# Transposes of a unit grouped over three PSUM banks, and two groups of heads at once in the halves of the partitions: a two-layer gated cross-attention kernel on one core

## The chip, the core and the metric

The kernel runs on one NeuronCore of one Trainium2 chip. The metric is the device time of one execution in microseconds (us), a median over runs. A core has TensorE (PE in the profile, its weight loads PEld), VectorE (DVE), ScalarE (ACT), GpSimd (POOL) and SyncE (SP, which here only issues DMAs). Each runs its own instruction stream in order, and they meet at semaphores.

## The reference, cut to what matters

```python
x = x + tanh(g_xattn[0]) * L0_xattn(layernorm(x), ctx, ...)          # "first attention"
x = x + tanh(g_ffn[0])   * L0_ffn(layernorm(x), ...)
x = x + tanh(g_xattn[1]) * L1_xattn(layernorm(x), ctx, ctx, ...)     # "second attention"
x = x + tanh(g_ffn[1])   * L1_ffn(layernorm(x), ...)
# L0_xattn: 2 batches, 256 queries, keys = 512 context rows + 256 latents, 32 heads of 128, 8 key heads,
#   q and k rms-normed; probs = softmax(q k^T / sqrt(128)); out = probs v; out @ Wo
# L1_xattn: 2 batches, 256 queries, 512 keys, 32 heads of 16, 8 key heads (4 heads share one);
#   softmax(q k^T / 4) v; out @ Wo
```

## The kernel before, in words

Matrices that need fp32 exactness are split into a high and a low part (hi by ScalarE, lo = value - hi by VectorE or GpSimd) and multiplied as three single-pass products (`mm3`, L70).

**First attention (`attn0`).** A loop of 8 turns g, one for each key head, which serves 4 query heads. In a turn a *unit* u is one query head h = u // 2 with one batch b = u % 2, 8 units. In iteration u of `attend` (L590) TensorE runs, in this order: at even u the transposes of the next head's queries ("q", 4 transposes into one bank), at odd u from 3 on the transposes that spread a head's softmax factors ("r", 4 of them), then the scores of unit u + 1 (12 matmuls), then three times four transposes of the probabilities of unit u ("p") followed by six matmuls with the values for unit u - 1 (`times_v`, L578). All groups of transposes go through two banks `tbank` in turn: a group c waits until VectorE has emptied the bank of group c - 2 (L536). ScalarE copies the high part out of the bank (L290) and takes the exponentials (L316), in the written order p, exp, p, exp, [o], p (L322 to L335), where o is the high part of a finished head's output (L310), at odd u from 3 on. VectorE takes row maxima (L443), subtracts for the low part (L430, L432) and scales a head's output with its factors (`normalise_o`, L452). The values' sums of a head alternate between two banks `obank`. GpSimd works through a fixed list in each turn (L223): low part of output 0 (L205), split of Wo, low part of output 1, split of the next turn's Wq (L183, L185), split of Wkv, and so on. TensorE's first projection of the next turn (`project_q`, L510) comes right after `attend` and waits for that split of Wq (L512).

**Second attention (`attn1`).** Here the contraction of a score is only 64 rows long: 16 dimensions times high and low parts of q and k. Rows 64 to 127 of `kS` and `qS` hold zeros (L780, L791), so each matmul covers 128 rows. A unit is one head and one batch, 64 units in all, in 4 turns of 16. For each TensorE makes the scores (2 matmuls of 512 columns, L1472) for the maxima (L1419); then it makes them again transposed, with the negated maxima added through an identity (4 + 4 matmuls of 256 columns, L1484 and L1489), which ScalarE exponentiates (L1400). Every fourth unit it multiplies four units with the values, in four groups of 32 columns of the array (L1503, 32 instructions of 256 columns), and transposes the result (L1512). ScalarE copies that result (L1390), VectorE divides it (L1441, L1443). `scores(n + 1)` stands ahead of `scores_T(n)` in TensorE's order (L1515 to L1525).

## Time and profile before

| | us |
|---|---|
| median of 3 runs | 1085.82 (1079.99 to 1086.55) |
| the profiled execution | 1088.03 |
| its span, first to last instruction | 1086.2 |
| TensorE busy | 1005.9 (93% of the span) |
| VectorE busy | 632.7 (58%) |
| ScalarE busy | 501.4 (46%) |
| GpSimd busy | 359.8 (33%) |
| mean granted TensorE clock | 0.975 of full speed |

Busy time is the time an engine spends in instructions, with waits left out. TensorE's matmuls are pipelined, so a matmul of 256 columns shows some 280 ns but starts some 117 ns after the one ahead of it: distances between starts tell its throughput, durations do not.

### The profile page before, as it was taken

What the parts mean: (1) busy time and instruction counts of PE and PEld (TensorE: products, weight loads), DVE (VectorE), ACT (ScalarE), POOL (GpSimd) and SP (SyncE); (2) the same over time, 40 slices, a digit from 0 to 9 for tenths busy, and PEclk for the clock granted to TensorE, in tenths of its full rate; (3) what the DMA queues carried; (4) which work ended last, traced back from release to release, by engine and by line L of the source; (5) the groups of instructions that cost most, each with busy time, mean ns of one, the idle gap of its engine ahead of it and who ended that gap; (6) DMA issues with size and microseconds to landing.
All of it is one profiled execution on the core that took longest, in us unless ns stands there. A gap on an engine that the chain in (4) does not pass through costs nothing. (4 is left out here: it accounts for less than half of the span.)

```text
span 1086.2 us, 18566 instructions
## 1 busy us (share of the span) xinstructions
PE 1005.9 (93%) x6748; PEld 878.6 (81%) x6748; DVE 632.7 (58%) x1102; ACT 501.4 (46%) x968; POOL 359.8 (33%) x246
## 2 busy tenths in 40 slices
PE   4899999999999999999999999999899969999975
PEld 3888989898898989889898898989677857777654
DVE  6566457556546745754674574567347736666464
ACT  4356337435534643653473374346145125555423
POOL 3307403720830371083046126305147308000041
PEclk9989999999999999999999999999999989999987
DMA  6001100200200110020011003000053072221001
GB/s 213 2 1 62 37 1 9 88 0 0 90 6 0 38 59 0 0 97 0 0 58 39 0 0 116 0 1 1 26 179 116 1 237 56 54 53 34 2 0 39
DMA packets 31409, 46.49 MB, mean 43 GB/s; under 512 B 3472, under 2 KB 15376, under 8 KB 31376
## 3 DMA queue, kind: packets, MB, share of 16 engines
q1 hardware_dynamic: 30800, 46.03, 13.6%
q8 instruction: 22, 0.36, 0.1%
q14 instruction: 11, 0.09, 0.0%
q10 hardware_dynamic: 576, 0.00, 0.0%
HBM read 41.83 MB, written 4.19 MB: 42 GB/s over the span
## 5 line engine op out<-in xcount | busy, mean ns | idle before, releaser
L430 DVE TENSOR_TENSOR ptL<-tbank,ptH 128x512 fp32r<-128x512 f32 x192 | 132.3, 689 | 84.0 <-ACT ptH L290 84.0
L290 ACT ACTIVATE ptH<-tbank 128x512 fp32r<-128x512 f32 x192 | 115.7, 603 | 109.5 <-PE tbank L539 109.2
L205 POOL TENSOR_TENSOR oTL<-o_norm,oTH 128x512 fp32r<-128x512 f32 x32 | 41.3, 1290 | 349.9 <-ACT oTH L310 349.9
L539 PE MATMUL tbank<-ident,probs 128*128 128x128 f32 x864 | 132.1, 275 | 16.5 <-DVE ptL L430 12.1
L443 DVE TENSOR_REDUCE negmax<-score 128x1 f32<-128x768 f32 x128 | 119.5, 949 | 19.9 <-PE score L74 19.9
L316 ACT ACTIVATE probs<-score,negmax 128x768 f32<-128x768 f32 x128 | 115.6, 904 | 15.5 <-DVE negmax L443 15.5
L72 PE MATMUL obank<-ptH,vH 128*128 128x256 f32 x384 | 122.3, 318 | 0.0
L401 DVE TENSOR_REDUCE sumsq<-probs 128x2 f32<-128x256 f32 (+1 forms) x80 | 42.0, 526 | 135.5 <-ACT probs L285 71.8
L539 PEld LDWEIGHTS tbank<-ident,probs 128*128 128x128 f32 x864 | 97.7, 140 | 26.5 <-DVE ptL L430 14.9
L74 PE MATMUL obank<-ptH,vL 128*128 128x256 f32 x384 | 108.8, 283 | 0.0
L1419 DVE TENSOR_REDUCE a_negmax<-a_score 128x1 fp32r<-128x512 f32 x128 | 82.3, 685 | 45.3 <-PE a_score L1472 44.5
L74 PE MATMUL score<-wkvH,kvT_lo 128*128 128x256 f32 x384 | 108.7, 283 | 0.0
L73 PE MATMUL score<-wkvL,kvT_hi 128*128 128x256 f32 x384 | 108.7, 283 | 0.0
L72 PE MATMUL score<-wkvH,kvT_hi 128*128 128x256 f32 x384 | 108.6, 283 | 0.0
L73 PE MATMUL obank<-ptL,vH 128*128 128x256 f32 x384 | 108.4, 282 | 0.0
L200 POOL TENSOR_TENSOR rnorm<-sumsq,neg_half 128x2 f32<-128x2 f32 (+1 forms) x80 | 71.4, 896 | 107.4 <-DVE sumsq L403 107.3
L1400 ACT ACTIVATE a_exp<-a_scoreT 128x1024 f32<-128x1024 f32 x64 | 65.6, 1025 | 60.2 <-PE a_scoreT L1489 60.2
L72 PE MATMUL score<-kTH,qTH 128*128 128x512 f32 (+1 forms) x256 | 92.4, 361 | 0.6 <-DVE kTL L430 0.6
L74 PE MATMUL score<-kTH,qTL 128*128 128x512 f32 (+1 forms) x256 | 87.2, 341 | 0.0
L73 PE MATMUL score<-kTL,qTH 128*128 128x512 f32 (+1 forms) x256 | 87.2, 341 | 0.0
L72 PEld LDWEIGHTS obank<-ptH,vH 128*128 128x128 f32 x384 | 73.6, 192 | 0.5
L72 PEld LDWEIGHTS score<-wkvH,kvT_hi 128*128 128x128 f32 x384 | 73.7, 192 | 0.3
(246 smaller groups left out, 2417.6 us busy)
## 6 DMA issues: line engine op xcount, KB each, us to landing
wqo_stage<-in_wq SPq DMA_DIRECT2D x9, 1024.0 KB, 5.6
wqo_stage<-in_wo SPq DMA_DIRECT2D x8, 1024.0 KB, 5.2
wkv_stage<-in_wkv SPq DMA_DIRECT2D x9, 512.0 KB, 6.4
a_qS<-q_scratch SPq DMA_DIRECT2D x24, 128.0 KB, 3.6
ctx_stage<-in_ctxT SPq DMA_DIRECT2D x2, 1024.0 KB, 12.5
kS<-k_scratch SPq DMA_DIRECT2D x32, 64.0 KB, 2.1
q_scratch<-qpart SPq DMA_DIRECT2D x16, 128.0 KB, 1.9
wqo_stage<-in_down_w SPq DMA_DIRECT2D x3, 512.0 KB, 3.5
```

The costliest lines, as they stand in the source:

```text
L72: pe.matmul(out, a[0], b[0], start=start, stop=False)
L73: pe.matmul(out, a[0], b[1], start=False, stop=False)
L74: return pe.matmul(out, a[1], b[0], start=False, stop=stop)
L200: pool.tensor_tensor(rn[:, GRP * it:GRP * it + n], ss[:, GRP * it:GRP * it + n], S.neg_half[:, 0:n], ALU.pow).then_inc(rn_done, 1)
L290: act.activation(out, tbank[c % 2][:], ACT.Copy, scale=scale).then_inc(t_hi, 1)
L316: act.activation(probs[:, m % NP, :], score[m % 2][:, 0:SKV], ACT.Exp, bias=negmax[:, m:m + 1], accum_out=rsum[:, m:m + 1]).then_inc(s_exp, 1)
L401: dve.tensor_reduce(ss[:, a:a + n], sq[:, it % 3, 0:n], AX.X, ALU.add).then_inc(ss_done, 1)
L430: i = dve.tensor_tensor(out, tbank[c % 2][:], f32(hi), ALU.subtract)
L443: dve.tensor_reduce(negmax[:, m:m + 1], score[m % 2][:, 0:SKV], AX.X, ALU.max, negate=True).then_inc(s_max, 1)
L539: i = pe.transpose(tbank[c % 2][:, n * P:(n + 1) * P], block_in, S.ident[:])
L1400: act.activation(expo[:, v % NE_, :], scoreT[v % 2][:], ACT.Exp).then_inc(s_exp, 1)
L1419: dve.tensor_reduce(negmax[:, 2 * (v % 2) + t:2 * (v % 2) + t + 1], score[t][:], AX.X, ALU.max, negate=True).then_inc(s_max, 1)
```

## The change

In the first attention the banks for transposes become three and `obank` one. The three groups of transposes of a unit follow each other, then come the three groups of matmuls with the values. The factors ("r") of a head move from odd u from 3 on to even u from 2 on, beside "q", with ScalarE's copy of them. A group of transposes now waits for the last user of its own bank (`place`, `user`): q has bank 1, r has bank 2, p has bank n % 3. Some waits and VectorE's order change with it, `NPT` goes from 4 to 5, and the last factors go ahead of the last matmuls with the values. GpSimd's low part of output 2 moves ahead of the split of Wkv.

In the second attention group 2i lies in rows 0 to 63 and group 2i + 1 in rows 64 to 127. A step m now holds one head of each, 32 steps. Score matmuls and the transposed ones take 64 rows each, written in pairs for the two halves and into different banks; the identity matmuls stay at 128 rows. `scores` has three banks, negated maxima a ring of 16; values are multiplied in two halves, one in each step; the loops are written out; the zero fills are gone; keys and queries of a turn are loaded a whole turn ahead, those of turn 1 ahead of the last feed-forward's weights. Cut to its core:

```diff
-    NP, NPT = 4, 4
...
-    tbank = [ps(f"tbank{i}", [P, 512], fp32) for i in range(2)]
-    obank = [ps(f"obank{i}", [P, 512], fp32) for i in range(2)]
+    tbank = [ps(f"tbank{i}", [P, 512], fp32) for i in range(3)]
+    obank = ps("obank", [P, 512], fp32)
+    wbank = [obank, tbank[2]]
...
-        if u % 2 == 1 and u >= 3:
-            order.append(("r", (u - 3) // 2))
+        if u % 2 == 0 and u:
+            order.append(("r", u // 2 - 1))
...
+    lows = {name: i for i, name in enumerate(name for name in order if name[0] != "r")}
+    TL = len(lows)
+
+    place = [n if kind == "p" and n < CH else {"p": n % CH, "q": 1, "k": c % 2, "r": 2}[kind] if c else 0
+             for c, (kind, n) in enumerate(order)]
+    user = [max((i for i in range(c) if place[i] == place[c]), default=None) for c in range(TC)]
...
+                o_lo_part(g, 2)
                 pool.wait_ge(pe_kv, NKV * g + NKV)
                 split_wkv(g + 1)
-                for h in range(2, GRP):
-                    o_lo_part(g, h)
+                o_lo_part(g, 3)
...
-                act.wait_ge(t_lo, TC * g + at["r", h] + 1)
+                act.wait_ge(o_scaled, GRP * g + h + 1)
...
-                    if u % 2 == 1 and u >= 3:
-                        factors(g, (u - 3) // 2)
+                    if u % 2 == 0 and u:
+                        factors(g, u // 2 - 1)
...
+                    if u % 2 == 1 and u >= 3:
+                        normalise_o(g, (u - 3) // 2)
                     if u + 1 < U:
                         maximum(g, 2 * u + 2)
                     if u % 2 == 0 and u // 2 + 1 < GRP:
                         lo_q(g, u // 2 + 1)
-                    if u % 2 == 1 and u >= 3:
-                        normalise_o(g, (u - 3) // 2)
                     if u + 1 < U:
                         maximum(g, 2 * u + 3)
+                    if u % 2 == 1:
+                        reciprocals(g, u // 2)
                     for c in range(CH * u, CH * u + CH):
                         lo(g, ("p", c), ptL[:, c % NPT, :], ptH[:, c % NPT, :])
-                    if u % 2 == 1:
-                        reciprocals(g, u // 2)
...
-                if c >= 2:
-                    pe.wait_ge(t_lo, TC * g + c - 1)
+                if name == ("p", 2):
+                    pe.wait_ge(t_lo, TL * g + lows["q", 1] + 1)
+                elif user[c] is not None:
+                    last_user = order[user[c]]
+                    if last_user in lows:
+                        pe.wait_ge(t_lo, TL * g + lows[last_user] + 1)
+                    else:
+                        pe.wait_ge(t_hi, TC * g + at[last_user] + 1)
...
-                if u % 2 == 0 and j == 0 and h >= 2:
-                    pe.wait_ge(t_lo, TC * g + at["r", h - 2] + 1)
-                pe.wait_ge(t_lo, TC * g + at["p", c] + 1)
+                if u % 2 == 0 and j == 0 and h:
+                    pe.wait_ge(o_scaled, GRP * g + h)
...
-                    if u % 2 == 1 and u >= 3:
-                        transpose_factors(g, (u - 3) // 2)
+                    if u % 2 == 0 and u:
+                        transpose_factors(g, u // 2 - 1)
                     if u + 1 < U:
                         scores(g, u + 1)
                     for j in range(CH):
                         transpose_probs(g, u, j)
-                        if u:
+                    if u:
+                        for j in range(CH):
                             times_v(g, u - 1, j)
             def finish_units(g):
+                transpose_factors(g, GRP - 1)
                 for j in range(CH):
                     times_v(g, U - 1, j)
-                transpose_factors(g, GRP - 1)
...
-            pool.memset(f32(S.kS[64:P, :, :]), 0.0).then_inc(k_zeroed, 1)
...
-            pool.memset(f32(S.qS[64:P, :, :, :]), 0.0).then_inc(S.q_zeroed, 1)
...
+    vcol = sb("a_vcol", [P, 2, 2, B * SCT, VW], fp32)
+    NX = 4
+    expo = sb("a_exp", [P, NX, 2, 2, 2, SQ], fp32)
...
+    NB = 3
...
+    obank = ps("a_obank", [P, 512], fp32)
...
+    NV = B * GRP
+    NM = NV * TURNS
+    NW = NM // 2
+    STACK = 16 * 16
+    half_rows = [slice(0, P // 2), slice(P // 2, P)]
...
+            for i in range(1, TURNS):
+                if i >= 2:
+                    sp.wait_ge(pe_sT, 2 * NV * (i - 1))
                 for s in range(2):
-                    sp.wait_ge(pe_sT, NU * i - U + U * s)
-                    S.load_k(sp, 2 * i + s, s)
-                    load_q(2 * i + s, s)
+                    S.load_k(sp, i, s)
+                    load_q(i, s)
+                if i == 1:
+                    ffn.loads(sp)
...
+            def exp(m, h):
+                act.wait_ge(pe_sT, 2 * m + h + 1)
+                if m >= NX and h == 0:
+                    act.wait_ge(pe_pv, (m - NX) // 2 + 1)
+                act.activation(expo[:, m % NX, h].rearrange("p s k q -> p (s k q)"), scoreT[h][:], ACT.Exp).then_inc(s_exp, 1)
+
+            def copy_o(w):
+
+                act.wait_ge(pe_pv, w + 1)
+                act.activation(o_quad[:, w % 2, :], obank[:, 0:SQ], ACT.Copy).then_inc(o_copied, 1)
+            for m in range(NM):
+                exp(m, 0)
+                if m % 2 == 1 and m >= 3:
+                    copy_o((m - 3) // 2)
+                exp(m, 1)
+            copy_o(NW - 1)
...
+            def windows(i):
+                for s in range(2):
+                    g = 2 * i + s
+                    dve.tensor_copy(vcol[:, i % 2, s, :, 0:D1], v_rows[:, :, g * D1:(g + 1) * D1]).then_inc(win, 1)
...
+            def maxima(m):
+
+                for e in range(4 * m, 4 * m + 4):
+                    dve.wait_ge(pe_s, e + 1)
+                    dve.tensor_reduce(negmax[:, e % 16:e % 16 + 1], score[e % NB][:], AX.X, ALU.max,
                                       negate=True).then_inc(s_max, 1)
...
+            windows(0)
+            maxima(0)
+            for m in range(NM):
+                if m % 2 == 0 and m >= 4:
+                    finish((m - 4) // 2)
+                if m + 1 < NM:
+                    maxima(m + 1)
+                if m % NV == 1 and m // NV + 1 < TURNS:
+                    if m // NV:
+                        dve.wait_ge(pe_pv, 4 * (m // NV))
+                    windows(m // NV + 1)
+            finish(NW - 2)
+            finish(NW - 1)
...
+            def scores(m, t):
+
+                i, b, j = unit(m)
+                if t == 0 and m % NV == 0:
+                    pe.wait_ge(stack_in[i % 2], STACK * (i // 2 + 1))
+                if t == 0 and m == GRP:
+                    pe.wait_ge(S.late_in[0], STACK // 2)
+                q = b * SQ + t * P
+                for s, rows in enumerate(half_rows):
+                    e = 4 * m + 2 * t + s
+                    if e >= NB:
+                        pe.wait_ge(s_max, e - NB + 1)
+                    pe.matmul(score[e % NB][:], qS[rows, i % 2, j, q:q + P], kS[rows, i % 2, b * SC:(b + 1) * SC],
+                              start=True, stop=True).then_inc(pe_s, 1)
+
...
+            def scores_T(m, h):
+
+                i, b, j = unit(m)
+                if m:
+                    pe.wait_ge(s_exp, 2 * (m - 1) + h + 1)
+                for k in range(2):
+                    key = b * SC + (2 * h + k) * P
+                    for s, rows in enumerate(half_rows):
+                        pe.matmul(scoreT[h][:, 512 * s + k * SQ:512 * s + (k + 1) * SQ], kS[rows, i % 2, key:key + P],
+                                  qS[rows, i % 2, j, b * SQ:(b + 1) * SQ], start=k == 0, stop=False)
+                pe.wait_ge(s_max, 4 * m + 4)
                 for t in range(2):
...
+                    for s in range(2):
+                        c = (4 * m + 2 * t + s) % 16
+                        x = pe.matmul(scoreT[h][:, 512 * s:512 * (s + 1)].rearrange("p (k q) -> p k q", k=2)[:, :, t * P:(t + 1) * P],
+                                      negmax[:, c:c + 1].to_broadcast([P, P]),
+                                      ident_r[:].unsqueeze(1).to_broadcast([P, 2, P]), start=False, stop=t == 1)
                 x.then_inc(pe_sT, 1)
...
+            def times_v(w, h):
+
+                i, b = w // 4, w % 4 // 2
+                if h == 0:
+                    pe.wait_ge(win, 2 * i + 2)
+                    if w:
+                        pe.wait_ge(o_step, 2 * w)
+                pe.wait_ge(s_exp, 2 * (2 * w + 1) + h + 1)
+                for k in range(2):
+                    for c in range(GRP):
+                        s, m = c // 2, 2 * w + c % 2
+                        x = pe.matmul(obank[VW * c:VW * (c + 1), 0:SQ], vcol[:, i % 2, s, b * SCT + 2 * h + k, :],
+                                      expo[:, m % NX, h, s, k, :], start=h == 0 and k == 0, stop=h == 1 and k == 1)
+                if h == 1:
+                    x.then_inc(pe_pv, 1)
+
...
+            for m in range(NM):
+                if m + 1 < NM:
+                    scores(m + 1, 0)
+                scores_T(m, 0)
+                if m >= 2:
+                    times_v((m - 2) // 2, m % 2)
+                if m + 1 < NM:
+                    scores(m + 1, 1)
+                scores_T(m, 1)
+                if m % 2 == 1 and m >= 3:
+                    transpose_o((m - 3) // 2)
+            for h in range(2):
+                times_v(NW - 1, h)
+            transpose_o(NW - 1)
...
+                    at, g = 64 * s + D1 * n, 2 * i + s
```

## Rows read from the trace of the kernel before

**Rows 1.** Windows by stage: stretch, its length, busy time of PE, PEld, DVE, ACT, POOL, PEclk, DMA
```profile
0.00:770.00 770.00, 722.81 (x4931) 660.23 (x4932) 453.69 (x782) 376.30 (x795) 279.18 (x173) 0.99 0.10 32
885.80:1027.50 141.70, 137.92 (x1184) 105.93 (x1184) 89.53 (x169) 71.76 (x80) 23.16 (x21) 0.97 0.26 62
1027.50:1086.20 58.70, 41.49 (x168) 29.31 (x168) 28.09 (x60) 17.90 (x33) 15.49 (x20) 0.81 0.05 18
```
**Rows 2.** Timeline of PE, iteration 1 of turn 4: start, us, engine, line, what
```profile
443.14 0.60 PE L539 MATMUL tbank<-ident,probs 128*128 128x128 f32 x4
443.49 0.36 PE L72 MATMUL obank<-ptH,vH 128*128 128x256 f32 x1
443.69 0.28 PE L73 MATMUL obank<-ptL,vH 128*128 128x256 f32 x1
...
444.29 0.60 PE L539 MATMUL tbank<-ident,probs 128*128 128x128 f32 x4
```
**Rows 3.** Timeline of PE: three of its stalls, in brackets, with who ended them
```profile
440.55 0.66 PE L539 MATMUL tbank<-ident,probs 128*128 128x128 f32 x4 [0.81 <-DVE ptL L430]
...
482.95 0.50 PE L72 MATMUL score<-wqH,kvT_hi 128*128 128x512 f32 x1 [1.73 <-POOL wqL L185]
...
769.27 0.47 PE L72 MATMUL obank<-woH,oTH 128*128 128x512 f32 x1 [3.56 <-POOL oTL L205]
```
**Rows 4.** Windows: iterations 0 and 1 of turn 4, and its `attend` whole
```profile
435.72:440.96 5.24, 4.22 (x29) 3.47 (x28) 3.88 (x6) 2.74 (x6) 0.00 (x0) 1.00 0.00 0
440.96:446.59 5.63, 5.63 (x45) 5.37 (x44) 4.35 (x6) 4.10 (x10) 0.00 (x0) 1.00 0.00 0
...
sum 47.23, PE 43.78 PEld 40.89 DVE 33.34 ACT 30.45 POOL 18.96; mean PE 5.47 PEld 5.11 DVE 4.17 ACT 3.81 POOL 2.37
```
**Rows 5.** Timeline of turn 4: an exponential of iteration 0; iteration 3's transposes p and their emptying
```profile
440.75 0.91 ACT L316 ACTIVATE probs<-score,negmax 128x768 f32<-128x768 f32 x1
...
455.16 0.60 PE L539 MATMUL tbank<-ident,probs 128*128 128x128 f32 x4
...
455.80 0.60 ACT L290 ACTIVATE ptH<-tbank 128x512 fp32r<-128x512 f32 x1 [1.94 <-PE tbank L539]
...
458.52 0.65 ACT L310 ACTIVATE oTH<-o_norm 128x512 fp32r<-128x512 f32 x1
...
459.04 0.61 ACT L290 ACTIVATE ptH<-tbank 128x512 fp32r<-128x512 f32 x1
...
459.69 0.69 DVE L430 TENSOR_TENSOR ptL<-tbank,ptH 128x512 fp32r<-128x512 f32 x1 [1.19 <-ACT ptH L290]
```
**Rows 6.** Timeline of POOL, turn 4
```profile
459.24 1.30 POOL L205 TENSOR_TENSOR oTL<-o_norm,oTH 128x512 fp32r<-128x512 f32 x1 [36.12 <-ACT oTH L310]
...
474.66 3.60 POOL L183 TENSOR_TENSOR wqH<-wqo_stage,zero 128x2048 fp32r<-128x2048 f32 x1 [2.04 <-DMA wqo_stage<-in_wq]
478.34 4.56 POOL L185 TENSOR_TENSOR wqL<-wqo_stage,wqH 128x2048 fp32r<-128x2048 f32 x1
```
**Rows 7.** Timeline, second attention: values' block, then the next unit
```profile
941.44 1.93 PE L1503 MATMUL a_obank<-a_exp,a_vcol 128*32 128x256 f32 x32
...
943.30 0.74 PE L1472 MATMUL a_score<-kS,a_qS 128*128 128x512 f32 x2
...
943.84 1.29 DVE L1419 TENSOR_REDUCE a_negmax<-a_score 128x1 fp32r<-128x512 f32 x2 [2.54 <-PE a_score L1472]
943.88 0.40 PE L1484 MATMUL a_scoreT<-a_ident_r,a_negmax 128*128 128x256 f32 x2
...
944.11 0.40 PE L1489 MATMUL a_scoreT<-a_qS,kS 128*128 128x256 f32 x2
```
**Rows 8.** Page, costliest groups: ScalarE's exponentials of the second attention
```profile
L1400 ACT ACTIVATE a_exp<-a_scoreT 128x1024 f32<-128x1024 f32 x64 | 65.6, 1025 | 60.2 <-PE a_scoreT L1489 60.2
```
**Rows 9.** Timeline of PE: the second attention's first identity matmuls and last values' block
```profile
888.78 0.63 PE L1484 MATMUL a_scoreT<-a_ident_r,a_negmax 128*128 128x256 f32 x2
...
1024.03 1.93 PE L1503 MATMUL a_obank<-a_exp,a_vcol 128*32 128x256 f32 x32 [1.20 <-ACT a_exp L1400]
```

More of the change, by code:

```diff
@@ L1386, in _ @@
         def _(act):
-            def copy_o(r, c):
-                act.wait_ge(pe_pv, r + 1)
-                act.activation(o_quad[:, c, :], obank[c][:, 0:SQ], ACT.Copy).then_inc(o_copied, 1)
-            def turn(i, first, last):
-                for v in range(NU):
-                    n, r = NU * i + v, QUADS * i + v // GRP
-                    if v % GRP == 2 and (not first or v >= GRP):
-                        copy_o(r - 1, (v // GRP - 1) % 2)
-                    act.wait_ge(pe_sT, n + 1)
-                    if v % GRP == 0 and (not first or v >= NE_):
-                        act.wait_ge(pe_pv, r - 1)
-                    act.activation(expo[:, v % NE_, :], scoreT[v % 2][:], ACT.Exp).then_inc(s_exp, 1)
-            turns(act, turn)
-            copy_o(QUADS * TURNS - 1, 1)
+            def exp(m, h):
[12 more added lines that the diff above has]
+            copy_o(NW - 1)
             for t in range(RT):
@@ L1422, in turn @@
-            def turn(i, first, last):
-                for v in range(NU):
-                    n, r = NU * i + v, QUADS * i + v // GRP
-                    if not (last and v == NU - 1):
-                        maxima(n + 1, (v + 1) % NU)
-                    if v % GRP == 3 and (not first or v >= GRP):
-                        finish_quad(i, r - 1, v // GRP - 1)
-                    if v == 4 and not first:
-                        dve.wait_ge(pe_pv, QUADS * i)
-                        window(2 * i + 1, 1)
-                    if v == 12 and not last:
-                        dve.wait_ge(pe_pv, QUADS * i + 2)
-                        window(2 * i + 2, 0)
@@ L1446, in _ @@
             dve.wait_ge(ones_set, 1)
-            window(0, 0)
-            window(1, 1)
-            maxima(0, 0)
-            turns(dve, turn)
-            finish_quad(TURNS - 1, QUADS * TURNS - 1, QUADS - 1)
+            windows(0)
[9 more added lines that the diff above has]
+                    windows(m // NV + 1)
@@ L1460, in _ @@
         def _(pe):
-            def scores(n, v, i):
-                s, b, j = unit(v)
-                if v % U == 0:
-                    pe.wait_ge(stack_in[s], STACK * i + STACK)
-                if isinstance(i, int) and i == 0 and b == 1 and j == 0:
-                    pe.wait_ge(S.late_in[s], 64)
-                for t in range(2):
-                    if not (isinstance(n, int) and n == 0):
-                        pe.wait_ge(s_max, 2 * n + t - 1)
-                    q = b * SQ + t * P
-                    pe.matmul(score[t][:], qS[:, s, j, q:q + P], kS[:, s, b * SC:(b + 1) * SC],
-                              start=True, stop=True).then_inc(pe_s, 1)
@@ L1511, in transpose_o @@
+            def transpose_o(w):
+                pe.wait_ge(o_copied, w + 1)
                 for t in range(2):
-                    x = pe.transpose(obank[c][:, SQ + t * P:SQ + (t + 1) * P], o_quad[:, c, t * P:(t + 1) * P], S.ident[:])
+                    x = pe.transpose(obank[:, SQ + t * P:SQ + (t + 1) * P], o_quad[:, w % 2, t * P:(t + 1) * P], S.ident[:])
                 x.then_inc(pe_oT, 1)
-            def turn(i, first, last):
-                for v in range(NU):
-                    n, r = NU * i + v, QUADS * i + v // GRP
-                    if not (last and v == NU - 1):
-                        scores(n + 1, (v + 1) % NU, i if v < NU - 1 else i + 1)
-                    scores_T(n, v, first)
-                    if not first or v >= GRP:
-                        if v % GRP == 1:
-                            times_v(r - 1, (v // GRP - 1) % QUADS, i if v >= GRP else i - 1, first)
-                        if v % GRP == 2:
-                            transpose_o(r - 1, (v // GRP - 1) % 2)
@@ L1526, in _ @@
-            pe.wait_ge(S.q_zeroed, 1)
-            scores(0, 0, 0)
-            pe.wait_ge(ident_set, 1)
-            turns(pe, turn)
-            times_v(QUADS * TURNS - 1, QUADS - 1, TURNS - 1, False)
-            transpose_o(QUADS * TURNS - 1, 1)
-            pe.wait_ge(o_step, 2 * QUADS * TURNS)
+            for t in range(2):
+                scores(0, t)
+            pe.wait_ge(ident_set, 1)
+            for m in range(NM):
[9 more added lines that the diff above has]
+                    transpose_o((m - 3) // 2)
```

143 lines of the change are left out of this document (47 added, 96 removed).

## The prediction, made before the changed kernel had run

> **What bounds the kernel now.** I read the stages first [rows 1]. The first attention fills 770 of 1086 us, and TensorE is busy in 94% of it; the second attention takes 142 us at 97%. So both edits are made where TensorE sets the pace, and the question is how much of its stream they shorten and which wait then ends last. Next I read TensorE's timeline by distances between starts. A group of four transposes takes 443.49 - 443.14 = 0.35 us, 0.088 each; the first matmul after it holds its successor for 0.20 where the next ones stand 0.12 apart, so going over from transposes to matmuls costs 0.09; the whole chunk, transposes and six matmuls, is 1.15 [rows 2]. In iteration 0 TensorE stalls because two banks don't suffice for three groups [rows 3]. At the end of a turn it waits again, 1.73 us, for GpSimd's split of Wq [rows 3]. That wait stands at 7 ends of turns, and it matters most: GpSimd's list runs from the first output's low part, started at 459.24, over the split of Wo, a reload and the split of Wq to 478.34 + 4.56 = 482.90 [rows 6], and TensorE resumes at 482.95. A turn can't hand over sooner than 23.8 us after the high part of output 0 ended (458.52 + 0.65, [rows 5]), however fast TensorE is. In the second attention VectorE's and ScalarE's shares are 63% and 51% [rows 1].
>
> **First attention, part by part.** *Switches.* Iterations 1 to 7 lose two switches each, and r now stands beside q, which saves two more: 16 x 0.09 = 1.44 us a turn. *Banks.* The three stalls on banks in `attend`, of which [rows 3] shows the largest, shrink. *The new wait.* r uses bank 2, and its last user is the third group p of the unit before. It must be emptied by ScalarE and VectorE. How long that takes is in [rows 5]: from the start of the first group, 455.16, to the end of the third low part, 459.69 + 0.69, 5.22 us; without the output's copy in between (458.52 to 459.04) 4.70. This chain doesn't get shorter when the groups stand together, since it is ScalarE's own p, exp, p, exp, o, p. But TensorE gets through faster: from its first group to the end of the iteration it now needs 3 x 0.35 + 0.09 + values. Values are 1.15 - 0.35 - 0.09 = 0.71 a chunk, 2.13 in all, sum 3.27. Then q 0.35 (with 0.1 of waiting), and r stands still: 4.74 - 3.72 = 1.0 us in iteration 2, 1.5 in iteration 4, and in iteration 6, which has no q, 5.26 - 3.27 = 2.0. Queued behind r on TensorE are the scores of the next unit, so nothing fills the gap.
>
> *The turn worked through*, from the start of q at 0. Scores take 443.14 - 440.96 = 2.18 after transposes, 2.09 otherwise [rows 2, 4]. Iteration 0: q and scores 2.53, first p 2.88, then a wait for q's low part to 3.36, two p to 4.06; the scores of iteration 1 wait for exponentials (the fourth ends at 440.75 + 0.91, 5.9 after the start, as before: same chain, [rows 5]) and end at 7.0; p 8.05, values 10.3. It was 5.24 + 5.63 = 10.87 [rows 4], so 0.6 gained. Iteration 2 is 0.35 + 0.1 + 1.0 + 0.35 + 2.18 + 3.27 = 7.25 (start of 3 at 17.5; before, 455.16 - 2.53 - 435.72 = 16.9, [rows 4, 5]), 3 is 2.09 + 3.27 = 5.36, 4 is 7.8, 5 is 5.36, 6 is 7.8 and ends at 43.8. In iteration 7 p waits for exponentials and for bank 2 to 45.7, the last values end at 48.1. GpSimd's list: the high part of output 0 comes 17.5 + 2.09 + 3.36 + 0.65 = 23.6 into the turn, before 23.45, so Wq is ready at 47.4 instead of 47.2. TensorE, formerly ready 1.7 ahead of it, now arrives 0.7 behind it. Instead of 47.23 [rows 4] a turn's `attend` takes 48.1: +0.9, and seven times +6. In the last turn no GpSimd waits and the loss is open: 48.1 - (47.23 - 1.73) = +2.6. There the earlier r takes its transposes and ScalarE's copy out of the 3.56 us stall ahead of the output [rows 3]: -0.6. Sum +8 us. Bounds: if r never stalls, GpSimd's list still holds the turn, and since its start would move up by at most the 1.0 of iteration 2 less 0.2, it is -0.8 x 7 = -6, less the last turn's 2: -8; with half a microsecond more a turn, +12.
>
> *Covered.* GpSimd's output 2 ahead of Wkv delays that split by 1.3 us (the length of output 0's, [rows 6]); the whole projection of q lies between and hides it. The zero fills lay in GpSimd's idle time: nothing. If either were not hidden, it would cost its own length, 1.3 us a turn or some 4 us once.
>
> **Second attention, part by part.** A step m stands for two units. TensorE per step: 8 identity matmuls at 0.117 = 0.94 (two in 0.23, [rows 7]); half a values' block, 0.86 to 0.93 (1.86 for 32 instructions with the way out, [rows 7]); transposes of outputs, 0.088 a step. Half-row matmuls are not in this trace; that column groups work at once is: 32 instructions in 1.86 are 0.058 each, where a full one of the same columns takes 0.117 [rows 7]. For a pair in two halves the bounds are the price of one (0.23 for 512 columns, 0.117 for 256) and of two. I take the lower for the 512 pairs, 0.46 a step, and for the four 256 pairs 0.176, two weight loads at the spacing of the transposes [rows 2], which are loads of 128 columns too: 0.70. Changes between full, half and column groups are five a step; 0.09 is known [rows 2], 0.15 the upper row value: 0.45 to 0.75. Sum 3.5 to 3.9.
>
> The Trainium skill, "TensorE: Matmul & The Clock Gate", section on LDWEIGHTS, gives a load its columns over 1.2 GHz, 107 ns for 128. The trace disagrees: load and transpose together stand 88 ns apart [rows 2]. By the page's figure the 256 pairs would take 0.85 a step and the gain of this stage would be some 15 us instead of 20, an estimate.
>
> *The chain.* The identity matmuls of step m + 1 need all four maxima of it, and the last two are asked for only in the middle of step m. From the first identity matmul: 0.47, change 0.09, half a block with the way out (1.86 - 0.15) / 2 + 0.15 = 1.0, scores to the first maximum 943.84 - 943.30 = 0.54, two maxima 1.29 [rows 7], 0.2 back to TensorE: 3.6 us. VectorE itself has 4 x 0.645 + 0.25 = 2.8, ScalarE 2 x 1.03 [rows 8] + 0.2 = 2.25. So the chain and TensorE are level; I take 3.6 a step. Before, 1024.03 - 888.78 = 135.3 for 31.5 steps [rows 9], 4.29. After: first identity 1.7 later (two more maxima, the fill of `a_vcol` twice as large), 31 x 3.6 less 1.8 for two steps without values and plus 1 for the start at the lower clock (two matmuls of 256 take 0.63 there, 0.40 later, [rows 7, 9]), then 4.7 to the end of the last block, 888.8 + 1.7 + 110.8 + 4.7 = 1006, against 1025.9: -20 us. Loads: 16 more DMAs ahead of the feed-forward's weights delay these by some 7 us; GpSimd has over 100 us of idle time behind them ([rows 1], POOL). The last stage is unchanged.
>
> **Sum.** 1088 - 20 + 8 = 1076 for the profiled execution, which lies 2.2 above the median; against the median 1085.8 - 12 = 1074.
>
> **Rivals.**
> 1. *Slower: the halves don't overlap, or each change drains the array.* Then a step is 0.94 + 0.86 + 0.09 + 0.92 + 0.94 + 0.5 to 0.75 = 4.3 to 4.5; 4.4 gives +3 there, with the first part +11: 1097. It decides from a step of 4.04 on, where the second part's gain is as large as the first part's loss. For it: no row here shows half rows, and the pairs alternate at 256 columns. Against: the column groups do overlap. The Trainium skill, "TensorEngine Tiling (Array Packing)", Key Properties, says that changing the mode drains the engine, which speaks for this rival; the way out of the values' block, which the trace shows in 1.86 us with its work, leaves room for some 0.15 us, not more.
> 2. *r does not stall as worked out* (ScalarE gets ahead), and GpSimd's list sets the turn: first part near 0 to -8, total 1058 to 1066, middle 1063. Against: the chain of [rows 5] is back to back.
> 3. *Loads and changes at their upper prices*, step 3.85: -12 + 8, 1081.
>
> **How the numbers follow.** Chances: the forecast 0.48 (its own range 1067 to 1081), rival 1 0.16, rival 2 0.18, rival 3 0.18. About 1% is what a measurement can tell from no change, 10.9 us: faster means below 1075. Of the forecast 0.28 lies below, all of rival 2, none else: 0.46. Slower, above 1096.7: 0.10 of rival 1, and 0.01: 0.11. Within: 0.43. The range 1060 to 1092 leaves out the lower third of rival 2 and most of rival 1.
>
> **What would show it.** Right: "r" transposes with 1 to 2 us of idle time in iterations 2, 4, 6, ended by VectorE's third low part; the wait for Wq gone or under 0.3; `attend` of a turn near 48; the second attention's steps 3.6 apart, negated maxima ending the wait of the identity matmuls. Wrong: steps above 4 with TensorE dense (halves in sequence), VectorE without gaps (its own bound, 2.9), or `attend` under 47.

## The result: 0.9% slower, where 1% faster was forecast

| | before | after |
|---|---|---|
| median of 12 runs each, us | 1083.68 (1079.99 to 1088.96) | 1092.58 (1091.15 to 1101.39) |
| the profiled execution, us | 1088.03 | 1093.26 |
| its span, us | 1086.2 | 1091.5 |
| mean granted TensorE clock | 0.975 | 0.977 |

The ratio is 1.0089, with a 95% interval of 1.0067 to 1.0112, which makes 9.7 us of 1085 (the medians differ by 8.9): a small loss, but clear of no change. The prediction of 1074 (1060 to 1092) has the wrong sign and its range just misses the time.

By stage, as [rows 1] has it for before. Windows of the changed kernel: stretch, length, busy time of PE, PEld, DVE, ACT, POOL, then PEclk and DMA.

```profile
2.14:786.12 783.98, 728.67 (x4928) 656.24 (x4929) 451.38 (x782) 375.16 (x795) 278.75 (x165) 1.00 0.09 32
...
902.65:1032.50 129.85, 127.90 (x1182) 86.11 (x1182) 89.79 (x167) 71.35 (x79) 23.53 (x21) 0.94 0.34 68
1032.50:1091.50 59.00, 40.17 (x170) 27.94 (x170) 28.60 (x62) 18.19 (x34) 15.53 (x20) 0.84 0.05 18
```

The last turn's output starts at 786.12 instead of 769.27 [rows 3]: the first attention lost 16.9 us (forecast +8). From the first scores to the end of the last values' block the second attention takes 129.9 instead of 140.0 us: it gained 10.1 (forecast 20). The rest is within 1.5 us. So the two forecasts missed by 8.9 and 9.9 us, and in the same direction; that the total lies so near to the range says little for them.

**First attention.** TensorE in turn 4 of the changed kernel:

```profile
449.50 1.47 PE L553 MATMUL tbank<-ident,probs 128*128 128x128 f32 x12
450.73 0.36 PE L72 MATMUL obank<-ptH,vH 128*128 128x256 f32 x1
...
452.97 0.60 PE L553 MATMUL tbank<-ident,q_rows 128*128 128x128 f32 x4
454.25 0.65 PE L553 MATMUL tbank<-ident,rsum 128*128 128x128 f32 x4 [0.69 <-DVE ptL L438]
...
457.67 1.09 PE L553 MATMUL tbank<-ident,probs 128*128 128x128 f32 x8 [0.21 <-DVE qTL L440]
...
468.13 0.65 PE L553 MATMUL tbank<-ident,rsum 128*128 128x128 f32 x4 [1.21 <-DVE ptL L438]
...
471.54 1.09 PE L553 MATMUL tbank<-ident,probs 128*128 128x128 f32 x8 [0.23 <-DVE qTL L440]
...
482.00 0.65 PE L553 MATMUL tbank<-ident,rsum 128*128 128x128 f32 x4 [1.65 <-DVE ptL L438]
...
492.20 0.39 PE L72 MATMUL score<-wqH,kvT_hi 128*128 128x512 f32 x1
```

To be seen: ahead of each r (`rsum`) an idle time ended by VectorE's low part, as predicted; ahead of the second group p a small one ended by `qTL`, which wasn't; at 492.20 no wait for GpSimd any more [rows 3]. The turn starts at 442.26, so `attend` takes 49.94 us, against 47.23 in [rows 4]. The waits of the changed kernel's TensorE between 300 and 800 us (total, times, longest):

```profile
PE tbank L553 <- DVE ptL L438: 18.1, 15, 1.8
PE tbank L553 <- DVE qTL L440: 3.3, 15, 0.2
PE obank L72 <- POOL oTL L213: 2.9, 1, 2.9
```

**Second attention.** TensorE over one step of two units and a bit more:

```profile
936.38 0.73 PE L1486 MATMUL a_scoreT<-a_ident_r,a_negmax 128*128 128x256 f32 x4
937.05 1.07 PE L1502 MATMUL a_obank<-a_exp,a_vcol 128*32 128x256 f32 x16
938.05 0.50 PE L1469 MATMUL a_score<-kS,a_qS 64*128 64x512 f32 x2
938.38 0.39 PE L1480 MATMUL a_scoreT<-a_qS,kS 64*128 64x256 f32 x4
938.71 0.73 PE L1486 MATMUL a_scoreT<-a_ident_r,a_negmax 128*128 128x256 f32 x4
939.28 0.38 PE L1511 MATMUL a_obank<-ident,a_o_quad 128*128 128x128 f32 x2
939.59 0.50 PE L1469 MATMUL a_score<-kS,a_qS 64*128 64x512 f32 x2
939.92 0.40 PE L1480 MATMUL a_scoreT<-a_qS,kS 64*128 64x256 f32 x4
940.25 0.73 PE L1486 MATMUL a_scoreT<-a_ident_r,a_negmax 128*128 128x256 f32 x4
940.92 1.07 PE L1502 MATMUL a_obank<-a_exp,a_vcol 128*32 128x256 f32 x16
```

No idle time stands in these rows: TensorE itself is the bound. From values' block to values' block it is 3.87 with output transposes (937.05 to 940.92) and 3.65 without, 3.76 on average; 3.6 was forecast. The two half-row scores and four half-row transposed scores take 0.66 us together (938.05 to 938.71), so the halves do overlap.

### The profile page after: what moved, and what is told of

Read it like the earlier page. It is cut to its first block and busy times, and to the rows that moved or that the text cites. A ratio compares the mean times of both kernels' runs of the same rounds, so it can differ in the third digit from the quotient of the medians.

```text
span 1091.5 us, 18222 instructions
## 1 busy us (share of the span) xinstructions
PE 1001.1 (92%) x6748; PEld 854.1 (78%) x6748; DVE 631.2 (58%) x1102; ACT 500.1 (46%) x968; POOL 355.5 (33%) x244
## 5 line engine op out<-in xcount | busy, mean ns | idle before, releaser
L553 PE MATMUL tbank<-ident,probs 128*128 128x128 f32 x864 | 116.8, 276 | 8.4 <-DVE qTL L440 7.9
L72 PE MATMUL obank<-ptH,vH 128*128 128x256 f32 x384 | 113.9, 297 | 0.0
## 6 DMA issues: line engine op xcount, KB each, us to landing
ctx_stage<-in_ctxT SPq DMA_DIRECT2D x2, 1024.0 KB, 13.7
```

Of the source, the lines that this page charges most:

```text
L72: pe.matmul(out, a[0], b[0], start=start, stop=False)
L553: i = pe.transpose(tbank[place[c]][:, n * P:(n + 1) * P], block_in, S.ident[:])
```

## The experiments

Where nothing else is said each timed run is given by its ratio to the kernel before, its 95% interval, and the microseconds that it makes of 1085.

**1. The two parts alone.** The attention functions of before and after were combined crosswise.

> Only the first attention's edits on the kernel before; the second attention is that of before. Theory (the loss of the changed kernel is all in the first attention, +16.9 us by the two profiles): 1084 + 15 to 17 = 1099 to 1101 us. By the prediction's own sum for this part (+8): 1092. Rival (the changed kernel's first attention costs this much only because something of the second was changed with it, for instance the place of the large buffers in memory): 1084 to 1090.

> Only the second attention's edits (with those of the feed-forward that feed it) on the kernel before. Theory: the step of two units is 3.76 us and the stage loses 10 to 12 us: 1072 to 1075 us. By the prediction's sum (-20): 1064. Together with the first-only kernel the two differences should add to that of the changed kernel, +9 us.

Measured: first only 1.0165 (1.0146 to 1.0183), +17.9 us; second only 0.9920 (0.9895 to 0.9945), -8.7. Together +9.2, where the changed kernel has +9.7; the second-only kernel's own trace has steps of 3.65 and 3.87 too. The stages add up, and each is to be explained by itself.

**2. The stall of r.**

```diff
-             place = [... {"p": n % CH, "q": 1, "k": c % 2, "r": 2}[kind] ...]
+             place = [... {"p": n % CH, "q": 1, "k": c % 2, "r": 0}[kind] ...]
```

> The changed kernel with the transposes of r in bank 0 instead of bank 2. Bank 0 was last used by the first group p of the unit before, which is empty long before. Theory (r's stall on bank 2 is the prediction's wait and costs 0.9, 1.4 and 1.9 us in iterations 2, 4 and 6): no idle time ahead of r, and a turn's attend falls from 49.9 towards GpSimd's list, which would be ready about 1 us earlier than now: 47.5 to 48.0, so 7 x 2.2 and about 3 in the last turn, in all 15 to 19 us less than the changed kernel, 1074 to 1078 us. Rival (r only shows a delay that ScalarE's chain imposes anyway; without it TensorE waits for the exponentials or the high part of p): below 4 us less, 1089 or more, with idle time ahead of p instead.

Measured: 0.9894 (0.9877 to 0.9912), -11.5 against before and 21 us less than the changed kernel, a little more than expected. Turn 4 of this kernel, PE, ACT and POOL:

```profile
443.37 0.60 PE L553 MATMUL tbank<-ident,rsum 128*128 128x128 f32 x4
...
452.56 0.60 ACT L298 ACTIVATE ptH<-tbank 128x512 fp32r<-128x512 f32 x1 [2.68 <-PE tbank L553]
...
455.28 0.64 ACT L318 ACTIVATE oTH<-o_norm 128x512 fp32r<-128x512 f32 x1
...
456.00 1.29 POOL L213 TENSOR_TENSOR oTL<-o_norm,oTH 128x512 fp32r<-128x512 f32 x1 [36.36 <-ACT oTH L318]
...
479.86 0.50 PE L72 MATMUL score<-wqH,kvT_hi 128*128 128x512 f32 x1 [1.50 <-POOL wqL L193]
```

r follows q at once (q started at 442.94), `attend` is 479.86 - 432.25 = 47.6, and GpSimd's split of Wq again sets the end of the turn. So the wait that the prediction named is the largest single loss, and one number in a list of banks takes it away.

**3. The low part of q.** In VectorE's `attend`:

```diff
+                     if u % 2 == 0 and u // 2 + 1 < GRP:
+                         lo_q(g, u // 2 + 1)
                      if u + 1 < U:
                          maximum(g, 2 * u + 2)
-                     if u % 2 == 0 and u // 2 + 1 < GRP:
-                         lo_q(g, u // 2 + 1)
```

> The changed kernel with VectorE's low part of q moved ahead of the first of the two maxima in its order. Theory (in iterations 2 and 4 the second group p waits 0.46 us for the low part of q, which stands behind a maximum of 0.9 us): this wait goes, about 0.9 us a turn, 5 to 7 us less than the changed kernel, if the stall of r right before doesn't set the iteration; the maximum is late by 0.7 us, but the exponentials have slack. Rival (the maximum, now 0.7 us later, makes the exponentials and then the emptying of the banks later, and the stall of r grows by as much): no difference, 1090 to 1095 us.

Measured: 1.0023 (1.0006 to 1.0041), 7 us less than the changed kernel. The waits for `qTL` are gone; iteration 0 waits 0.7 us for an exponential instead. This is the loss that the prediction missed.

**4. GpSimd's list as the next bound.** The bank 0 kernel shows where the list can start earlier: ScalarE idles 2.7 us ahead of the first group p of iteration 3 (row 452.56), while VectorE had the output ready at 451.2; its high part is copied only at 455.28. The first kernel has both edits above; the second also moves `hi_o` ahead of `hi_p(g, CH * u)` in ScalarE's `attend`.

> The changed kernel with r in bank 0 and VectorE's low part of q ahead of the maximum, and ScalarE's copy of the output where it was: the kernel with the early list without its third edit. Theory (without r's stalls GpSimd's list sets the turn, so TensorE's time saved elsewhere is only waited away at the end of the turn): the same as with r in bank 0 alone, 1071 to 1074 us, with 0.5 us or so more of waiting for Wq at the end of each turn; only the last turn gains. Rival (TensorE's own time still counts): 5 us less, 1067 to 1069.

> The changed kernel with three edits to orders in the first attention: r in bank 0, VectorE's low part of q ahead of the maximum, and on ScalarE the high part of a finished output ahead of the first group p of its iteration instead of behind the second exponential. In the kernel with r in bank 0 alone TensorE waits 1.5 us at the end of a turn for GpSimd's split of Wq, ScalarE stands idle for 2.7 us in front of that group p, and the normalised output is ready 4 us before ScalarE copies it. Theory (with the stalls of r gone, GpSimd's list sets the turn; it starts with that copy): the list starts 4 us earlier and TensorE's own time sets the turn, 47.5 - 1.5 - 0.7 = 45.3 us for attend instead of 47.5, 7 x 2.2 and 1 more in the last turn below the r-in-bank-0 kernel (1073.6): 1056 to 1060 us. Rival (the list's end is set by the reload of Wq or by the output's other parts): TensorE still waits for Wq, 1068 to 1073 us.

Measured: without the move 0.9870 (0.9832 to 0.9907), -14.1, hardly more than with bank 0 alone, and the waits for Wq between 300 and 800 us (four turns) rise from 5.3 to 7.4 us; with it 0.9698 (0.9665 to 0.9732), **-32.8 us, a median of 1051.1 us, better than both kernels**. Turn 4 (it starts at 421.89), PE, ACT and POOL:

```profile
440.91 0.63 ACT L318 ACTIVATE oTH<-o_norm 128x512 fp32r<-128x512 f32 x1 [1.36 <-DVE o_norm L464]
441.15 1.47 PE L553 MATMUL tbank<-ident,probs 128*128 128x128 f32 x12
441.62 1.28 POOL L213 TENSOR_TENSOR oTL<-o_norm,oTH 128x512 fp32r<-128x512 f32 x1 [32.35 <-ACT oTH L318]
...
460.74 4.60 POOL L193 TENSOR_TENSOR wqL<-wqo_stage,wqH 128x2048 fp32r<-128x2048 f32 x1
...
466.77 0.39 PE L72 MATMUL score<-wqH,kvT_hi 128*128 128x512 f32 x1
```

The list starts 19.7 us into the turn instead of 23.8, Wq is ready 1.4 us ahead of TensorE, and `attend` is 44.9 us.

**5. Does a change between transposes and matmuls cost anything?** The same kernel with the grouping undone: three banks, but each group of four followed by its chunk of values.

> The kernel with the three edits (r in bank 0, low part of q first, early high part of the output), with the grouping of the transposes undone: each group of four is again followed by the six matmuls of a values' chunk; three banks stay. Theory (a change between transposes and matmuls costs TensorE nothing, the 0.09 of the prediction was a misreading: four transposes and six matmuls take 4 x 0.109 + 6 x 0.117 = 1.14 us in either order): the same time as the grouped kernel within 3 us, iterations of odd units equal within 0.1 us. Rival, as the prediction had it (14 more changes of 0.09 a turn, with two groups of q and r as they are): 8 x 1.3 = 10 us longer.

Measured: 0.9775 (0.9743 to 0.9807), 8.4 us more than grouped. By the time alone the prediction's saving of 10 us would be shown; the rows say otherwise. From the first p of iteration 2 to that of iteration 3 it is 445.29 - 439.74 = 5.55 us by chunks (the first two rows), and 441.15 - 435.59 = 5.56 grouped (the third; 441.15 stands above):

```profile
439.74 0.60 PE L553 MATMUL tbank<-ident,probs 128*128 128x128 f32 x4
445.29 0.60 PE L553 MATMUL tbank<-ident,probs 128*128 128x128 f32 x4
```

```profile
435.59 1.47 PE L553 MATMUL tbank<-ident,probs 128*128 128x128 f32 x12
```

The loss stands in the last iteration of a turn. By chunks, the waits between 300 and 800 us have a line that the grouped kernel lacks, and turn 4 shows one of them:

```profile
PE obank L72 <- DVE o_norm L464: 5.5, 5, 1.2
```

```profile
467.89 0.68 DVE L464 TENSOR_TENSOR o_norm<-obank,o_norm 128x512 f32<-128x512 f32 x1
...
468.62 0.39 PE L72 MATMUL obank<-ptH,vH 128*128 128x256 f32 x1 [1.08 <-DVE o_norm L464]
```

The output has one bank now, and the next head's values may not start before it is read. With the groups together all three of them stand in between; by chunks only one does. The whole trace has 8 such waits, 8.7 us in all, and a turn takes 91.65 instead of 90.83 us, which over 8 turns is 6.6 of the 8.4; the intervals are wide enough for the rest. So grouping is worth 8 us here as cover for the single output bank, and nothing as a saving of changes: both orders take 1.15 us a chunk.

**6. The changes of mode in the second attention.** On the second-only kernel: `scores_T` with the loops swapped so that each half's two matmuls stand together (`for s ... for k` instead of `for k ... for s`); and the same with each half's two identity matmuls directly behind, which makes four more changes between half and full rows a step.

> The second-attention-only kernel with the four transposed-score matmuls of 256 columns ordered by halves of the rows (first half twice, then the second half twice) instead of in alternation. Theory (neighbours in different halves overlap, 4 in 0.33 us, neighbours in the same half don't): two of four follow in their own half, so 0.02 to 0.12 us more for each of two groups a step, +1 to +8 us against the 1076.4 of the second-only kernel. Rival (the halves don't overlap in these matmuls, only their loads count): no difference, within 1 us.

> The second-attention-only kernel, with the transposed scores of the one half of the rows, then its four... two identity matmuls, then the scores of the other half and their two identity matmuls: four more changes between half rows and full rows in a step of two units than in the kernel that does the two halves after each other without a break. Theory (each change costs TensorE 0.19 us): 4 x 0.19 = 0.76 us more a step than that kernel, 32 x 0.76 = +24 us. Rival (a change costs little; the sum of the step is long for another reason): under +5 us.

Measured: half by half 0.9874 (0.9836 to 0.9911), not longer than second-only (0.9920, intervals overlap), step unchanged at 3.65 and 3.87; with the identity matmuls between 1.0321 (1.0257 to 1.0386), 48 us more than half by half, steps 4.89 and 5.11. TensorE half by half, with the same distances as in alternation (938.05, 938.38 and 938.71 above):

```profile
938.32 0.50 PE L1454 MATMUL a_score<-kS,a_qS 64*128 64x512 f32 x2
938.66 0.40 PE L1465 MATMUL a_scoreT<-a_qS,kS 64*128 64x256 f32 x4
938.99 0.73 PE L1471 MATMUL a_scoreT<-a_ident_r,a_negmax 128*128 128x256 f32 x4
```

And with the identity matmuls between:

```profile
934.42 1.07 PE L1486 MATMUL a_obank<-a_exp,a_vcol 128*32 128x256 f32 x16
935.43 0.49 PE L1454 MATMUL a_score<-kS,a_qS 64*128 64x512 f32 x2
935.76 0.40 PE L1465 MATMUL a_scoreT<-a_qS,kS 64*128 64x256 f32 x2
936.09 0.50 PE L1470 MATMUL a_scoreT<-a_ident_r,a_negmax 128*128 128x256 f32 x2
936.52 0.50 PE L1465 MATMUL a_scoreT<-a_qS,kS 64*128 64x256 f32 x2
936.95 0.50 PE L1470 MATMUL a_scoreT<-a_ident_r,a_negmax 128*128 128x256 f32 x2
937.38 0.50 PE L1454 MATMUL a_score<-kS,a_qS 64*128 64x512 f32 x2
```

Each lone pair of 256-column matmuls holds the next for 0.43, and two at pace are 0.235 [rows 7]: a change costs 0.19. Four of them are 0.76; and the second half's pair now has nothing to overlap with, twice 0.235 = 0.47; sum 1.23 a step, measured 1.24. Over 32 steps that is 40 of the 48 us; this kernel also had the low clock for 34.1 us instead of 20.5 (experiment 7), some 5 us at the price found there. My theory had only the first term. The expectation on the order within the four was wrong as well: the time is that of one half's own matmuls, in whichever order the two halves' are written.

The changes around the values' block cost a little less. The trace's single starts stand in fours, 0.216 us from four to four, so the 16 instructions are 0.86 of work. From the identity matmuls ahead of the block to the scores behind it are 938.05 - 936.38 = 1.67, less 0.47 for the identity matmuls and 0.86: 0.34 is left for two changes, 0.17 each. With these numbers the changed kernel's step is 8 identity matmuls 0.94, values 0.86, scores and transposed scores 2 x 0.467, three changes between half and full rows 0.57, two around the values 0.34, output transposes 0.11: 3.75 against 3.76 in the trace.

> The early-list kernel with the second attention's values of a quad in one block of 32 matmuls every second step, where the changed kernel does half of it in every step. Everything else of the step is in the same order; one change of TensorE's mode less in two steps (4 + 5 instead of 5 + 5). Theory (a change costs 0.19 us each): 15 x 0.19 = 3 us less, 1049. Rival (the chain of the maxima, now without a half block between the two pairs of scores in even steps, ends last there and TensorE waits for the negated maxima): no gain, or up to +5 us, with idle time ahead of the identity matmuls in even steps.

The edit: `if m % 2 == 1 and m >= 3`, both halves of `times_v((m - 3) // 2, h)`. Measured: 0.9688 (0.9658 to 0.9717), which can't be told from the 0.9698 without it. In its trace two steps take 7.41 instead of 7.52. That is 0.11, not the 0.19 of the theory; by the prices above, one change between full and half rows takes the place of two around the values, 0.34 - 0.19 = 0.15. In all it is some 2 us, and this execution had a longer stretch at the low clock than the one it is compared with (23.9 us for 20.5, below).

**7. The low clock at the start of the second attention.** In all profiles but that of the fill kernel below TensorE's granted clock falls to 0.5, the lower of its two levels (1.2 GHz), in the 7 us of TensorE's idle time at the end of the feed-forward stage, and rises some time into the second attention. Windows of 4 us that begin 7 to 8 us after the first scores (at 902.65 and 886.02), first of the changed kernel, then of the kernel before:

```profile
910.00:914.00 4.00, 4.00 (x20) 2.98 (x18) 1.98 (x4) 2.00 (x2) 0.00 (x0) 0.50 1.08 161
```

```profile
894.00:898.00 4.00, 4.00 (x28) 3.28 (x27) 3.40 (x7) 2.62 (x4) 0.00 (x0) 1.00 0.99 248
```

> The changed kernel once more, for its profile. In its first profile the granted clock is 0.5 for 15.8 us after TensorE's first scores of the second attention, in the kernel before for 6.5 us. Theory (the longer stretch belongs to the changed stage and took some 4 us of its gain): 12 to 20 us again. Rival (the stretch varies from one execution to the next whatever the kernel): anything from 5 to 20 us, unlike the first.

> The changed kernel a third time, as the run before: theory 12 to 20 us at clock 0.5 after the first scores, rival anything from 5 to 20.

> The kernel before once more, for its profile. Theory (the stretch at the low clock is short where the matmuls cover all rows): 5 to 8 us after the first scores, as in the first profile (6.5) and in the first-only kernel (6.6). Rival (it varies whatever the kernel): over 9 us.

> The kernel before with the first attention of the early-list kernel (the change with its three mended orders) and the old second attention. Theory (the two stages add up): 1052 + 9 = 1061 us, so that banks and grouping in the first attention are worth 24 us once the waits they bring are taken away; low clock at the start of the second attention 5 to 8 us as with the other old second attentions. Rival (the mended first attention is faster only through what follows it): 1055 or less, or 1068 or more.

Summed over windows of 1 us, the clock was low for 10.2 us in all four profiles with the old second attention (two of before, first-only, mended first), and for 20.5 us in all three of the changed kernel. These sums begin in the idle time; from the first scores on it is 5.9 to 7.4 us with the old stage and 16.6 to 17.0 in the changed kernel, as the theories had it. So the longer stretch belongs to the changed stage, and the rival falls, though the length isn't fixed by the stage alone: of the other kernels with the new stage five had 20.5 as well, three 13.7, one 17.1, the one with whole blocks 23.9, the one with four more changes 34.1. Its price: from the first scores to the last transposed scores the five with 20.5 and the changed kernel took 126.0 to 126.9 us, two with 13.7 took 123.8 and 124.1, about 2.4 us less for 6.8, so the 10.3 us by which the changed stage is low for longer cost some 3.6, an estimate. The mended first attention with the old second: 0.9808 (0.9770 to 0.9846), -20.8 us, which with -8.7 gives -29.5 for the pair (measured -32.8, within the intervals).

> The early-list kernel (1052 us) with 54 transposes of the identity, results unused, at the end of TensorE's work in the feed-forward stage: there it has finished and stands idle for 7.0 us until the block ends, and the granted clock falls to 0.5 during that idle time. Theory (the clock falls because TensorE is idle, and once low it stays low some 15 us into the second attention where the half-row matmuls are, against 7 us in the kernel before): the clock stays at 1.0 through the start, the first steps take 3.8 instead of 4.6 us, 4 to 6 us less: 1046 to 1048. Rival (the clock falls anyway, or the fill ends late and holds up the start): no difference or +1 to +3 us.

The edit: 54 times `pe.transpose(bank[6][:, 0:P], S.ident[:], S.ident[:])` at the end of TensorE's work in `ffn0`. Measured: 0.9699 (0.9671 to 0.9727), no difference. The clock did stay at 1.0 through the filled time, but fell about 2 us after the first scores, and was low for 13.7 us, all of them behind the first scores, where without the fill it is 16.7. The first scores came 8.4 us after the last projection instead of 7.0, probably because the fill, which ends 5.9 us after the projection, held the end of the block back. The small gain and the delay cancel.

> The early-list kernel with VectorE's low part of q ahead of the maximum in iterations 2 and 4 only, behind it in iteration 0 as in the changed kernel. With it ahead everywhere TensorE waits 0.7 us in iteration 0 for an exponential, with it behind 0.2 us for the low part and 0.3 for the exponential. Theory (what ends iteration 0 is the chain of maxima and exponentials, which starts 0.7 us earlier this way): 0.1 to 0.5 us a turn less, 1 to 4 us. Rival (the chain is the same length either way): within 1 us.

Measured: 0.9707 (0.9678 to 0.9737), no difference from 0.9698. The waits move from the exponential to the low part of q, and the rival holds.

## Why the prediction was wrong, step by step

- **r's stalls** (first attention, the new wait): right in place and nearly in size. q to r starts 1.28 and 1.80 us apart where 0.44 would do, so 0.8 and 1.4, and 1.8 in iteration 6; forecast 1.0, 1.5, 2.0. Bank 0 removed them and 21 us.
- **The saving of 1.44 us a turn by fewer switches**: this step failed; the switches cost nothing, where 0.09 each was taken. I had read 0.35 us to the matmul after four transposes and 0.20 from that to the next as a price of 0.09 for going over [rows 2]. A group of twelve shows the pace: (1.47 - 0.27) / 11 = 0.109 each, and four at that pace and six matmuls at 0.117 are the 1.14 of a chunk with no switch at all. The first matmul is merely recorded early. So the transposes cost 0.109 each where 0.088 was taken. Experiment 5 found equal iterations in either order. With it went the sum of each iteration: odd ones take 5.57 where I had 5.36.
- **The wait for the low part of q**: this step failed by omission. The sum had such a wait in iteration 0 and none in iterations 2 and 4, without a reason. There the second group p needs the bank that VectorE empties of q, behind a maximum of 0.96 us. It starts 0.81 and 0.83 us after the first group where 0.44 would do, some 0.4 us each; the even iterations took 7.79 and 8.30 instead of 7.25 and 7.8. Experiment 3: 0.90 a turn, 7 us.
- Together they make `attend` 49.94 us instead of 48.1: 0.9 of the 1.84 is the low part of q, the rest mostly the slower transposes, with which an odd iteration alone is 0.2 longer. Seven times +1.84 is 12.9 above the forecast, and the last turn takes 56.2 us to its output instead of 51.9, +4.3 where +2 was forecast: 15.2 us above it in all, against the 8.9 measured. Some 5 are given back because the profile of before, and not that of the changed kernel, has three stretches of 3.4 us at the low clock inside the first attention (two whole turns with one of them took 1.6 us longer), and turn 4, on which I had built the sum, has none; another 1.3 because the part of a turn behind `attend` got 0.19 shorter. The output's last stall shrank from 3.56 to 2.95, the forecast 0.6.
- **GpSimd's list** was read rightly as a floor (rival 2's reason): with r out of the way TensorE waits 1.5 us for Wq again, and only an earlier start of the list opens it.
- **Changes of mode** (second attention): the term that was mis-sized. Five at 0.09 to 0.15 were taken; three cost 0.19 and two 0.17, 0.91 instead of 0.45 to 0.75. The 0.15 that I put down to the way out of the values' block stands in no row: the block's 1.86 us are 1.73 of work (eight fours at 0.216) and 0.13 of the change, whose other part falls on the first matmul behind it. The values themselves were right, 0.86. The transposed scores went the other way, 0.23 instead of 0.35 per group of four, since they overlap as well as the others do. The Trainium skill, "TensorEngine Tiling (Array Packing)", Key Properties, says that a change of mode drains the engine. The runs agree that a change holds TensorE up, here by 0.17 to 0.19 us each. That half of rival 1 was nearer to the runs than the forecast; its other half, that the halves don't overlap, was not.
- **The pace of 0.088 a weight load**, put against the Trainium skill's 107 ns for 128 columns ("TensorE: Matmul & The Clock Gate", section on LDWEIGHTS): for transposes the trace agrees with the page, 0.109 measured, and my reading of [rows 2] was wrong by the same misreading as the switch. For the half-row pairs neither figure came out: a step's eight loads and matmuls take 0.47 us, where 0.70 was forecast and 0.85 was the estimate by the page's figure.
- **The second attention's -20**: the stage came out at -10.1 because TensorE's own step was underestimated and the low clock lasted longer. The step of 3.76 instead of 3.6 costs 31 x 0.16 = 5.0, the longer low clock 3.6, the end of the last block 1 us more (5.7 for 4.7): 9.6 of the missing 9.9.
- Of the rivals, the third (changes at their upper prices) came nearest for the second attention: its step of 3.85 was too long and its gain of 12 still too large, since it had no longer low clock. The first rival's 1097 is nearer to the measured time than the forecast, but by luck: its step of 4.4 didn't occur, and the halves do overlap. None had the first attention at +17.

Why the clock stays low for longer in the changed stage is not settled. Filling the idle time before it only moved and shortened the stretch. Kernels whose second attention is the same had 13.7, 17.1 and 20.5 us, the one with fewer changes of mode 23.9 and the one with more 34.1, so neither the stage alone nor the number of changes orders them. The window at 910.00 shows TensorE busy for all of its 4.00 us. No run here separates half rows, changes of mode and what went before.

## What to carry to other kernels

A new bank is worth what its slowest user allows: put a group into the bank whose last user is emptied earliest, and walk through every engine's order for what now stands ahead of the emptying; here one bank number and two moved lines turned +9.7 us into -32.8. Take the price of a repeated change (transposes to matmuls, full to half rows) from the pace of a long group, not from the gap to the next record, and test a claimed saving on an iteration without waits: the 8 us that grouping did bring came from a cover for one output bank. And look for the engine whose list sets the floor and start it earlier; time saved elsewhere is otherwise waited away.

## What the runs showed of the hardware that was not expected

- Half-row matmuls in the two halves of the array overlap fully: two of 512 and four of 256 columns take 0.66 us with one change, 0.467 without it, which is the price of one half's share (0.235 for one of 512 columns and 0.235 for two of 256); the order in which the halves' matmuls are issued doesn't matter.
- Each change between half rows and full rows holds TensorE for 0.19 us, each of the two around a block in groups of columns some 0.17; one between transposes and matmuls over the full array costs nothing, 1.15 us a chunk in either order.
- TensorE's clock stood at the lower level for 10.2 us around the start of the old second attention in all four profiles, and for 13.7 to 34.1 us with the new one.
